# The last output projection and the decision tree of a decoder joined into one program of 17 steps

## The reference, cut to what matters

```python
out = jnp.einsum(... ctx, Wo) + bo            # cross-attention, layer 1
x = _layernorm(x + out)
...
q = jnp.einsum('btd,ed->bte', x, Wq)
gate = jax.nn.sigmoid(q_flat @ routers.T)      # (tokens, 255)
leaf_prob = _leaf_probs(gate)                  # product of 8 branch probabilities
ret = (leaf_prob @ leaf_values).reshape(Bv, Tv, d)
out = jnp.einsum('btd,ed->bte', ret, Wout_w) + Wout_b
x = _layernorm(x + out)
```

## Time and profile before

| | us |
|---|---|
| median of three runs | 1533.96 |
| lowest and highest | 1533.04, 1535.55 |
| the profiled execution | 1535.46 |
| its span, first to last instruction | 1533.7 |
| last projection t4 within the span | 1433.9 to 1474.2 |
| tree within the span | 1474.45 to the end |

### The profile page before, as it was taken

The page is one execution under the profiler, slowest core; times in us unless marked ns, Lnnn a source line. Parts: engine busy times, 40 slices in busy tenths (PEclk is TensorE's granted clock), DMA queues, the critical chain, the costliest instruction groups (busy, mean ns, idle before and its releaser), DMA issues. The chain is left out here.

```text
span 1533.7 us, 24876 instructions
## 1 busy us (share of the span) xinstructions
PE 1382.1 (90%) x9358; PEld 753.1 (49%) x9358; DVE 1068.5 (70%) x2336; ACT 759.4 (50%) x1027; POOL 337.0 (22%) x425
## 2 busy tenths in 40 slices
PE   6996899999999979658998889999999999999976
PEld 3664488847898966313335413333333333332555
DVE  3797466661121238668995789999999999993547
ACT  1442366611111102325764316787788877788432
POOL 2110322251000037633336320000000000000241
PEclk9998899999999989959999859999999999999998
DMA  9754533366898822764422541422234322220001
GB/s 343 243 176 143 150 133 124 119 225 211 280 300 276 301 67 63 216 201 116 137 64 78 154 157 27 99 70 65 65 80 101 79 66 65 70 60 1 1 1 55
DMA packets 153353, 198.69 MB, mean 130 GB/s; under 512 B 16235, under 2 KB 125311, under 8 KB 153106
## 3 DMA queue, kind: packets, MB, share of 16 engines
q1 hardware_dynamic: 141516, 165.34, 35.8%
q0 software_dynamic: 9200, 29.64, 6.2%
q10 hardware_dynamic: 2518, 2.13, 0.4%
HBM read 136.08 MB, written 60.70 MB: 128 GB/s over the span
## 5 line engine op out<-in xcount | busy, mean ns | idle before, releaser
L2089 DVE TENSOR_REDUCE xa_part<-psum 128x1 f32<-128x512 f32 (+1 forms) x768 | 471.3, 672 | 27.6 <-PE psum L1942 25.5
L2041 ACT ACTIVATE xa_P<-psum 128x1024 f32<-128x1024 f32 (+1 forms) x416 | 403.3, 1020 | 110.1 <-PE psum L1966 109.8
L1966 PE MATMUL psum<-sa_Q,xa_K 48*128 48x512 bf16 (+3 forms) x1664 | 265.7, 381 | 4.0 <-DMA sa_Q<-xa_mrow 2.9
L1942 PE MATMUL psum<-xa_K,sa_Q 48*128 48x512 bf16 (+1 forms) x768 | 242.0, 394 | 4.4 <-DVE xa_part L2089 2.3
L1982 PE MATMUL psum<-xa_P,xa_V 128*32 128x512 f32 (+1 forms) x1664 | 222.6, 607 | 0.4 <-ACT xa_P L2041 0.4
L1942 PEld LDWEIGHTS psum<-xa_K,sa_Q 48*128 48x128 bf16 x768 | 59.2, 94 | 241.5 <-DVE xa_part L2089 174.1
L1966 PEld LDWEIGHTS psum<-sa_Q,xa_K 48*128 48x128 bf16 (+3 forms) x1664 | 101.9, 97 | 78.0 <-ACT xa_P L2041 20.9
L2086 DVE CUSTOM_DVE_ANT_0 psum<-psum,cf_sb 128x512 f32<-128x512 f32 (+3 forms) x256 | 119.5, 522 | 25.7 <-PE psum L1942 25.0
L1295 PEld LDWEIGHTS psum<-xtT,wgu 128*128 128x128 f32 x992 | 115.5, 192 | 5.8 <-issue 4.6
L1295 PE MATMUL psum<-xtT,wgu 128*128 128x128 f32 x992 | 115.9, 275 | 1.4 <-issue 0.8
L2041 ACT ACTIVATE sa_P<-psum 128x1024 f32<-128x1024 f32 (+3 forms) x128 | 83.4, 702 | 44.0 <-PE psum L1966 43.8
(11 more groups left out here) (238 smaller groups left out, 2128.2 us busy)
## 6 DMA issues: line engine op xcount, KB each, us to landing
wgu<-in_f_gu SPq DMA_DIRECT2D x31, 1024.0 KB
xa_K<-kx SPq DMA_DIRECT2D x192, 100.1 KB, 4.9
wdn<-in_f_dn SPq DMA_DIRECT2D x31, 512.0 KB
vx<-xv_v SPq DMA_DIRECT2D x48, 256.0 KB, 3.5
xa_V<-vx POOLq DMA_DIRECT2D x16, 768.0 KB, 6.4
sa_Q<-qs SPq DMA_DIRECT2D x64, 96.0 KB, 2.3
sa_K<-ks SPq DMA_DIRECT2D x64, 96.0 KB, 2.3
sa_Q<-qx SPq DMA_DIRECT2D x64, 96.0 KB, 2.3
```

The lines of the kernel that those rows point to most:

```text
L1942: last = pe.matmul(out[:, 0:width], hb.q(u)[tile:tile + HALF, to, qt * P:(qt + 1) * P], hb.k(u)[tile:tile + HALF, to, cut[e]:cut[e] + widt ...
L1966: last = pe.matmul(out(j), hb.k(u)[tile:tile + depth, to, kt * P:kt * P + r], hb.q(u)[tile:tile + depth, to, q0(kt):L], start=(half == 0), ...
L2041: act.activation(Pr[0:r, (u * KT + kt) % PR, h:h + 2, 0:w_], S_PS(p)[0:r, :, 0:w_], ACT.Exp, scale=SCALE).then_inc(s_exp, 1)
L2089: dve.tensor_reduce(part[:, g % 2, col + qt, e:e + 1], src[:, 0:cut[e + 1] - cut[e]], AX, ALU.max).then_inc(s_1free, 1)
```

## The change

heads_tail is no longer called for t4, and l1_tree is replaced by l1_out, one block with both. It has 17 steps. In step s the projection does what it did before in step c. The gates of chunk s-4, leaves of two chunks when s-5 is odd, and the tree's Tail from chunk s-7 follow it. A chunk's gates are now two tiles, in one bank (5), so there are eight groups of 8 matmuls and 16 sigmoids of 510 columns. The weight products are made in step 1. The banks are: 0 and 1 by_query, 2 and 3 input and output of the projection, 4 its matmuls (one place in place of two), 5 the logits, 6 the tree's input, 7 its matmuls (one place each). Tail gets `slots`, the number of places of each PSUM ring; cT, r and the other SBUF rings stay at two. GpSimd's queue is interleaved: residual and power of the projection, power of the tree, residual of the tree. VectorE's order in a step is contexts, projection's apply, sum and statistics, tree's apply, leaves, tree's sum and statistics. The diff also adds dve_offset and act_apply to Tail, which nothing calls. The core of the diff:

```diff
-    def __init__(self, env, c, name, banks, tiles, kc, behind=0, inputs=True, copied=False):
+    def __init__(self, env, c, name, banks, tiles, kc, behind=0, inputs=True, copied=False, slots=None, scaled=False):
...
+        self.slots = slots or (ring, ring, ring)
...
-        at = self.banks[which] * BANK + c % self.ring * width
+        at = self.banks[which] * BANK + c % self.slots[which] * width
...
-        self.free(pe, self.s_cT, c)
+        self.free(pe, self.s_cT, c, self.slots[0])
...
-        self.free(pe, self.s_pr or self.s_r, c)
+        self.free(pe, self.s_pr or self.s_r, c, self.slots[1])
...
-        self.free(pe, self.s_xT, c)
+        self.free(pe, self.s_xT, c, self.slots[2])
...
-def l1_tree(nc, env):
+def l1_out(nc, env, OT, wo, bo, bv):
...
+    PER = TB // len(PAIR_TILES(0))
+    GATES, LEAVES, TREE, END = 4, 5, 7, 9
+    STEPS = CHUNKS + END
...
-        tail = Tail(env, c_, "t5", (2, 4, 6), PAIR_TILES, KD)
+        proj = Tail(env, c_, "t4", (2, 4, 2), PAIR_TILES, KD, behind=3, slots=(2, 1, 2))
+        tree = Tail(env, c_, "t5", (6, 7, 5), PAIR_TILES, KD, slots=(1, 1, 1))
...
+                for s in range(STEPS):
+                    if s < CHUNKS:
+                        for t in PAIR_TILES(s):
+                            by_query(t)
+                    if at(s, 3) is not None:
+                        pe.wait_ge(proj.s_cT, min(s, CHUNKS))
+                        proj.pe_out(pe, s - 3)
+                    if at(s, 1) is not None:
+                        proj.pe_proj(pe, s - 1, lambda k: wo[:, k, :])
+                    if s == 1:
+                        for n, (a, b_, width) in enumerate((("d_wq", "d_rT", NG), ("d_lvT", "d_woT", D))):
...
+                    if at(s, GATES) is not None:
+                        gates(s - GATES)
+                    if at(s, TREE + 1) is not None:
+                        tree.pe_proj(pe, s - TREE - 1, lambda k: lw[:, k, :])
+                    if at(s, TREE) is not None:
+                        c = s - TREE
+                        tree.pe_in(pe, c, lambda i: leaf[:, c // PER % 2, c % PER * 2 + i, :],
+                                   lambda i: pe.wait_ge(s_leaf, c // PER + 1))
+                    if s < CHUNKS:
+                        proj.pe_in(pe, s, lambda i: cx[:, (2 * s + i) % 4, :], lambda i: pe.wait_ge(s_cx, 2 * s + i + 1))
...
+                for s in range(STEPS):
+                    if at(s, 3) is not None:
+                        proj.act_out(act, s - 3)
+                    if at(s, GATES) is not None:
+                        gates(s - GATES)
+                    if at(s, TREE) is not None:
+                        tree.act_in(act, s - TREE)
+                    if s < CHUNKS:
+                        proj.act_in(act, s)
...
+                for s in range(STEPS):
+                    if s < CHUNKS:
+                        proj.pool_residual(pool, s, lambda t: bo)
+                    if at(s, 1) is not None:
+                        proj.pool_rstd(pool, s - 1)
+                    if at(s, TREE + 1) is not None:
+                        tree.pool_rstd(pool, s - TREE - 1)
+                    if at(s, 4) is not None:
+                        pool.wait_ge(proj.s_xT_ps, s - 3)
+                        tree.pool_residual(pool, s - 4, lambda t: w["d_bout"])
...
+                for s in range(STEPS):
+                    if s < CHUNKS:
+                        for t in PAIR_TILES(s):
+                            context(t)
+                    if at(s, 2) is not None:
+                        proj.dve_apply(dve, s - 2)
+                    if at(s, 1) is not None:
+                        proj.dve_sum(dve, s - 1)
+                        proj.dve_stats(dve, s - 1)
+                    if at(s, TREE + 2) is not None:
+                        tree.dve_apply(dve, s - TREE - 2)
+                    if at(s, LEAVES) is not None and (s - LEAVES) % PER == PER - 1:
+                        leaves((s - LEAVES) // PER)
+                    if at(s, TREE + 1) is not None:
+                        tree.dve_sum(dve, s - TREE - 1)
+                        tree.dve_stats(dve, s - TREE - 1)
...
-            heads_tail(nc, env, "t4", OT, env.w["x_wo"], env.w["x_bo"], env.w["x_bv"])
-        l1_tree(nc, env)
+            l1_out(nc, env, OT, env.w["x_wo"], env.w["x_bo"], env.w["x_bv"])
```

More of the change, by code:

```diff
@@ L215, in dve_apply, with dve_offset, act_apply @@
         last.then_inc(self.s_xn, 1)
+    def dve_offset(self, dve, c):
+        u = c % self.ring
+        dve.wait_ge(self.s_rstd, c + 1)
+        dve.scalar_tensor_tensor(self.nm[:, u, :], self.mv[:, u, :, 0], -1.0, self.rstd[:, u, :],
+                                 ALU.mult, ALU.mult).then_inc(self.s_nm, 1)
+    def act_apply(self, act, c):
+        u = c % self.ring
+        act.wait_ge(self.s_nm, c + 1)
+        for i, t in enumerate(self.tiles(c)):
+            last = act.activation(self.env.x[:, t, :], self.r[:, u, i, :], ACT.Identity, bias=self.nm[:, u, i:i + 1],
+                                  scale=self.rstd[:, u, i:i + 1])
+        last.then_inc(self.s_xn, 1)
     def dve_norm(self, dve, c):
@@ L2315, in gates, with by_query @@
[L2315 to L2321, removed]
+                def by_query(t):
+                    b, i = divmod(t, TB)
+                    if t >= 2:
+                        pe.wait_ge(s_cx, t - 1)
+                    for g in range(G):
+                        last = pe.transpose(O_PS(t)[:, g * P:(g + 1) * P], OT[:, b * G + g, i * P:(i + 1) * P], env.ident)
+                    last.then_inc(s_ops, 1)
@@ L2322, in gates @@
+                def gates(c):
+                    pe.wait_ge(proj.s_xT, c + 1)
+                    if c == 0:
+                        pe.wait_ge(s_w, 2)
+                    else:
+                        pe.wait_ge(s_og, c)
+                    for i, t in enumerate(PAIR_TILES(c)):
+                        for k in range(KD):
+                            last = pe.matmul(G_PS[:, i * M:i * M + NG], env.xT[:, k, t * P:(t + 1) * P], wr[:, k, 0:NG],
                                              start=(k == 0), stop=(k == KD - 1))
@@ L2323, in gates @@
                     last.then_inc(s_gps, 1)
-                gates(0)
-                for c in range(CHUNKS + 1):
-                    if c % TC == 0 and c // TC + 1 < B:
-                        gates(c // TC + 1)
-                    if c >= 1:
-                        tail.pe_proj(pe, c - 1, lambda k: lw[:, k, :])
-                    if c < CHUNKS:
-                        tail.pe_in(pe, c, lambda i: leaf[:, c // TC % 2, c % TC * TC + i, :],
-                                   lambda i: pe.wait_ge(s_leaf, c // TC + 1))
+                pe.wait_ge(s_bvb, 1)
@@ L2390, in leaves @@
                     last.then_inc(s_leaf, 1)
[L2392 to L2399 removed]
+                dve.tensor_copy(bvb[:, :, :], bv.unsqueeze(2).to_broadcast([P, KD, P])).then_inc(s_bvb, 1)
+                dve.wait_ge(s_bps, 1)
+                dve.tensor_tensor(bo, B_PS, bo, ALU.add).then_inc(s_bias, 1)
+                for s in range(STEPS):
[14 more added lines that the diff above has]
+                        tree.dve_stats(dve, s - TREE - 1)
             @block.sync
```

98 lines of the change are left out of this document (56 added, 42 removed).

## The result

| | before | after |
|---|---|---|
| median of four runs, us | 1534.14 | 1525.37 |
| lowest and highest | 1533.04, 1535.55 | 1524.57, 1526.4 |
| profiled execution, its span | 1535.46, 1533.7 | 1526.4, 1524.7 |
| from the start of the copy to t_bvb to the start of the last apply | 96.52 | 87.52 |

The account below looks back on a forecast made before the run. In-order DVE was taken as the bound, 4.23 us a projection step. Projection later +10.05, new stretch from sum(7) to the last apply +44.3, old one -61.9: -7.55 from 1533.96, so 1526.4 us; range 1521.5 to 1531.5.

Parts of the forecast that it names:

- Part 1: Weight products moved into step 1, between pe_proj(0) and pe_in(1) on PE: sum(1) comes 2.3 us later, at 1447.0.
- Part 2: One accumulator bank for the projection: the wait for the sum before is met as it comes, 1.6 us to spare.
- Part 3: Gates in steps 4 to 7: a loop through PE and ACT takes 6.1 us a step, sum(7) comes at 1479.3.
- leaves(0): DVE's leaf products beside POOL's residual adds: 1.5 us longer, but DVE has 1.5 to spare, so no cost.
- Part 4: From sum(7) to the last apply's end: 44.3 us, DVE the bound; tree applies 0 to 3 beside POOL's adds 1.48 each.
- The half clock: Tree's pe_proj(3) and pe_proj(5) run slow after PE's idles in steps 11 and 13: +0.3 and +1.15 us.
- Cheap ends: Rival: the clock stays full (-1.45) and the applies cost 1.12 (-1.4), 1523.5 us; chance 0.15.
- Half clock to the end: Rival: from step 13 on every group of pe_proj takes 3.8 us, 1530.0 us in all; chance 0.15.
- the half clock of steps 8 to 11: Rival: PE's clock falls in step 8 and stays at 1.2 GHz through step 11, 1542.3 us, slower by 8; chance 0.05.
- Part 5: What goes: the wait at the tree's head, as gates and sigmoids run under the projection, and the block between the programs.

Follow-up runs that it names:

- a3: Changed kernel with the weight products spread over steps 0 to 3 in place of all in step 1: copy to last apply 87.55 us, median 1525.01 us.
- b1: Kernel before with one accumulator bank for the projection's matmuls and one bank for the tree's input: ratio 1.0003, copy to last apply 96.52 us.
- a4: Changed kernel with the tree's bias added by PE in PSUM instead of by GpSimd: copy to last apply 88.18 us, median 1525.68 us.
- c3: Changed kernel with GpSimd's adds for tree chunks 4 to 7 moved under the statistics, ahead of the power: copy to last apply 87.18 us, median 1519.86 us.
- a5: Changed kernel with ten unused matmuls on PE in step 12: copy to last apply 86.33 us, median 1524.35 us.
- a2: Changed kernel with the projection's pe_in and act_in ahead of the gates and sigmoids: copy to last apply 88.85 us, median 1523.9 us.
- a7: Changed kernel with the tree's steps two later: copy to last apply 90.17 us, median 1525.58 us.
- a6: Changed kernel with the tree's steps five later: copy to last apply 91.93 us, median 1527.3 us.
- a1: Changed kernel with leaves ahead of the tree's apply in VectorE's order: copy to last apply 84.97 us, median 1521.75 us.
- c4: Changed kernel with a1, c3, nine unused matmuls in step 12, and a2's order in steps 4 to 6: copy to last apply 81.47 us, median 1518.24 us.
- c2: Changed kernel with leaves ahead of the tree's apply and nine unused matmuls in step 12: copy to last apply 84.58 us, median 1522.85 us.

## Why the prediction was right, point by point

**What is right.** The time, 1526.4 forecast and 1525.37 measured, and the way there. The new stretch from sum(7) to the last apply's end was to take 44.3 us and takes 43.85 (1478.26 to 1522.1); the loss in front of it was 10.05 and is 9.06 (1478.26 less 1469.25, and 0.05 for the earlier start). The two differences, 1.0 and 0.45, are the 1.45 by which the gain is larger: 9.0 in the trace. Of the 44.3, 0.15 are a slip: 0.64 behind apply(5) at 1515.9 is 1516.55 and not 1516.7 for sum(6).

**Part 1.** sum(1) forecast at 1447.0, measured 1446.93. As a state it holds; as a cost of the place it is 0.3 (a3), since PE catches up before the gates. I should have asked how much of PE's work lies ahead of gates(0), not when one step ends.

**Part 2.** Nothing for the projection, shown by b1.

**Part 3, the mis-sized term.** The loop from gates to gates is there: PE waits 0.43, 0.41 and 0.42 for cT in steps 5 to 7. I took 6.1 and it is 5.82. ScalarE:

```profile
1461.57 1.15 ACT L2405 ACTIVATE og<-psum 128x510 f32<-128x510 f32 x2 [2.79 <-PE psum L2360]
1462.60 0.60 ACT L153 ACTIVATE t_cT<-psum 128x512 f32<-128x512 f32 x1
```

The sigmoids begin 1.92 behind the gates' start (1459.65), cT starts 1.03 behind them and not 1.2 (its row begins 0.12 before theirs ends), and takes 0.60. So sum(4) came at 1459.85 (1460.3) and sum(5) at 1465.67 (1466.4). The whole loop is 1.92, 1.03, 0.65, 0.49 and 1.73 from start to start, 5.82; I had added durations where the starts lie closer.

**leaves(0).** I took 1.5 us for the adds beside it; it is 1.2 (4.59 from 1467.55 to 1472.14, less the 3.36 of the earlier trace rows). That DVE had 1.5 to spare there did not hold: step 8 was to wait for PE's pe_proj(7) at 1479.15, and PE had that done at 1477.8. sum(7) followed DVE's own apply(6), which the lock had lengthened to 1.54 as well. In a4, where 0.4 of the first and all of the second are gone, sum(7) comes 43.99 behind the copy instead of 44.41 and waits 0.72 for PE: the two paths are that close, and the lock costs 0.4 up to there. My working had an apply beside POOL's adds only behind sum(7).

**Part 4.** tree sum(0) was to come 5.2 behind sum(7), it is 5.21. The apply beside two adds was to hold up the next operation by 1.48; it is 1.46 (1490.56 to 1492.02), four times behind sum(7), while a4 and c3 show applies of 0.73 and 0.74 without the adds. The Trainium skill, page "SBUF — State Buffer", section "Who interferes with whom", says that an operation of tensor_scalar's kind in its two-port mode and a GpSimd operation exclude each other for whole instructions and that the one issued first goes first. The traces agree on who goes first: GpSimd's adds start 0.07 earlier (1490.49 and 1490.56), take 1.46 where they take 1.40 alone, and the apply ends just behind them. For the whole instruction they don't show it: the two together last 1.61 us (1490.49 to 1492.10), while 1.40 and 0.73 one behind the other would be 2.13; the ends of GpSimd's rows are rough.

**The half clock.** pe_proj(5): 1.15 forecast, a wait of 1.12 measured, and a5 shows that its removal gives 1.2. pe_proj(3) was to be slow and was not, in three executions (3.44, 3.45 and, in a5, 3.45 of idle); it was in a2 and a3 with the same idle, and in a3 it cost the 0.3 that I had put down for it (a wait of 0.32). The forecast was a rule from one row, idle 2.85 and then 3.78; this case shows that such a row tells what can happen and not what will. That pe_proj(6) was not slow as well is partly luck: in a7 and c3 it was, and it cost 1.9 more.

**Rivals.** Cheap ends had two conditions: the applies cost in full, and one of two groups kept the clock. Half clock to the end and the half clock of steps 8 to 11 did not come: PE waited 1.34 for cT(7) and stayed at the full clock. That gates can run at half the clock is shown by a2, whose gates(3) did (3.46) behind an idle of 2.15, and then recovered; no run had it for several steps.

**Part 5.** That gates and sigmoids run under the projection is half of the gain. By a6, 4.6 us are gained with no gates under it at all: the weight products moved ahead (5.87) and the start without waiting for the projection's end (1.48), less what the two-tile gates and the steps behind them lose (1.51 and 1.25). I had not split these.

## What to carry to other kernels

When two in-order programs are merged, lay out one step of every engine and look for loops that cross engines and come back (gates, sigmoids, cT, pe_out): the loop sets the pace before any engine's busy time does, and an operation belongs ahead of the one that can be late, not behind it. Work that is moved earlier on an engine that can catch up before its next tight place costs nothing; ask for the sum of work up to that place. Compare edits by section and not by totals: a2, a1, c3 and a5 gave -1.33, 2.55, 0.34 and 1.19 us alone, 2.75 in sum, and c4, which joins most of them, 6.05. But the totals of a1 and c3 hold the luck of the clock in the last section (0.75 and -1.90), and that of a2 a step 7 that c4 leaves as it was. Section by section the gains add up: 0.78, then 1.79 and 2.24, then 1.22 are 6.03.

## What was not expected of the hardware

- PE's pe_proj(3) had the full clock behind 3.44 and 3.45 us of idle in two executions of the changed kernel and in a5, and the half clock behind 3.45 in two variants. In one of them, a3, PE's order differs only in steps 0 to 3, some 40 us earlier. What sets it there is open. Before pe_proj(5), where the changed kernel has 5.18 us of idle, no variant without unused matmuls had the full clock all through (idle 4.27 and 2.88 for the group in a1; 4.60 and 3.75 in c3; 2.75 and 3.65 in a3, behind two slow groups).
- 18 or 20 unused matmul instructions in the idle time keep the full clock (a5, c2, c4), at no cost to the other engines that the traces show.
- GpSimd's own adds lose next to nothing when they start first: 1.46 beside the applies, 1.40 alone. Beside the wide products of leaves(0), of which one was running when they started, two adds took twice as long in the changed kernel:

```profile
1469.96 2.84 POOL L130 TENSOR_TENSOR x_sb<-x_sb,x_bo_sb 128x256 f32<-128x256 f32 x2
```

- Sums from PSUM and the statistics are not lengthened beside GpSimd's adds. In the changed kernel the adds from 1459.54 to 1461.00 stand beside a sum of 0.69 and statistics of 0.75, and in c3 statistics beside adds keep 0.75.
